# The embedding of an early-fusion kernel: positions and image products ahead of the feature products, epsilon on ScalarE, a fourth group of gathers at the start, large loads behind the first gathers

## The reference

```python
# image tokens: 16x16 patches of x, a product, the bias, a position
patches = conv(pixel_values, conv_w, strides=(16, 16)) + conv_b
h_image = patches + pos_table[pos_ids]
# text tokens: eight numbers of a table by token, powers 0 to 4 of them, a product, a position
x = turns[input_ids]                       # 8 numbers for each token
powers = x[..., None] ** arange(5)         # 40 features for each token
emb = einsum('bstp,tpd->bsd', powers, poly_coeffs) + pos_table[:s]
h_text = (emb - mean(emb)) * rsqrt(var(emb) + 1e-12) * ln_gamma + ln_beta
h = concatenate([h_image, h_text], axis=1)
# what follows begins with a normalization of every token
xn = (h - mean(h)) / sqrt(var(h) + 1e-5)
```

## Time and profile before

| | us |
|---|---|
| median of three runs (1141.53 to 1149.68) | 1148.24 |
| the profiled execution, its own time | 1145.32 |
| its span on the core | 1143.4 |
| end of the embedding in it | 95.0 |
| first instruction of the next stage in it | 95.3 |

### The profile page before, as it was taken

How to read it: one execution, slowest core, us unless ns; L and a number is a source line. 1 busy time by engine, 2 the same in 40 slices (tenths; PEclk the granted TensorE clock), 3 DMA queues, 4 the chain that set the end, 5 groups by cost and what they waited for, 6 DMA issues and landing times. The chain is left out here.

```text
span 1143.4 us, 22929 instructions
## 1 busy us (share of the span) xinstructions
PE 748.7 (65%) x6119; PEld 519.3 (45%) x6120; DVE 948.8 (83%) x2473; ACT 778.6 (68%) x1335; POOL 162.6 (14%) x271
## 2 busy tenths in 40 slices
PE   4761167765888456666666666666643298799997
PEld 3641023533555233333333333333322186688996
DVE  5876878787888799999999999999999872476676
ACT  0342045875888789999999999999974065345553
POOL 5840030006554000000000000000000740000000
PEclk9995579997999778787787777777755687899999
DMA  5001000001111111001010000000003000455542
GB/s 163 3 2 69 0 0 1 0 0 29 36 36 37 38 23 22 21 21 21 21 22 21 21 21 21 21 21 21 14 6 145 11 1 1 178 186 179 199 174 100
DMA packets 84368, 54.59 MB, mean 48 GB/s; under 512 B 53832, under 2 KB 83304, under 8 KB 84072
## 3 DMA queue, kind: packets, MB, share of 16 engines
q1 hardware_dynamic: 83304, 53.97, 15.4%
q0 software_dynamic: 1024, 0.13, 0.2%
HBM read 11.77 MB, written 3.76 MB: 14 GB/s over the span
## 5 line engine op out<-in xcount | busy, mean ns | idle before, releaser
L1281 DVE SCALAR_TENSOR_TENSOR expo<-expo,con,pow 128x153 f32<-128x153 f32 x480 | 146.1, 376 | 0.7 <-ACT expo L1215 0.7
L1110 PE MATMUL at_pT<-identb,vi 128*128 128x128 bf16 x480 | 62.8, 299 | 88.4 <-ACT vi L1189 87.9
L1094 PE MATMUL at_rem<-below,identb 128*128 128x459 bf16 x160 | 68.2, 426 | 61.6 <-ACT expo L1215 60.9
L1215 ACT ACTIVATE expo<-at_rem,con 128x459 f32<-128x459 f32 x160 | 96.7, 641 | 15.3 <-PE at_rem L1095 7.6
L923 DVE TENSOR_REDUCE rs_ends<-rs_banks 128x770 f32 (+1 forms) x96 | 91.2, 959 | 15.9 <-PE rs_banks L894 14.9
L843 ACT ACTIVATE rs_banks<-rs_banks 128x770 f32<-128x770 f32 x96 | 76.4, 798 | 26.5 <-PE rs_banks L886 25.0
L1178 ACT ACTIVATE octave<-at_banks,con 128x459 int16<-128x459 f32 x160 | 90.2, 652 | 1.3 <-PE at_banks L749 0.2
L744 PE MATMUL at_banks<-pick,row_top 128*128 128x459 bf16 x160 | 78.4, 490 | 18.7 <-ACT octave L1178 17.0
L1330 DVE CUSTOM_DVE_ANT_0 weight_top<-weight_top,line 128x2448 uint16<-128x2448 uint16 x64 | 83.8, 1350 | 8.3 <-ACT line L1206 5.2
L1110 PEld LDWEIGHTS at_pT<-identb,vi 128*128 128x128 bf16 x480 | 44.3, 133 | 102.0 <-issue 76.4
L1306 DVE TENSOR_TENSOR expo<-expo,inv_total 128x1224 f32<-128x1224 f32 x64 | 83.6, 1347 | 0.0
(11 more groups left out here) (390 smaller groups left out, 2217.1 us busy)
## 6 DMA issues: line engine op xcount, KB each, us to landing
qk<-vt SPq DMA_DIRECT2D x64, 384.0 KB, 3.1
rs_kb<-qk SPq DMA_DIRECT2D x128, 28.7 KB, 2.0
kb<-qk SPq DMA_DIRECT2D x128, 28.7 KB, 1.9
patches<-in_patches SPq DMA_DIRECT2D x4, 768.0 KB
vi<-vt SPq DMA_DIRECT2D x32, 96.0 KB, 2.0
out<-vi SPq DMA_DIRECT2D x32, 96.0 KB, 1.8
pj_w<-in_w SPq DMA_DIRECT2D x1, 2304.0 KB, 8.1
qb<-qk SPq DMA_DIRECT2D x128, 6.0 KB, 1.8
```

What stands on the lines that cost most here:

```text
L1094: pe.matmul(out, identb[:, :], bank(below, b), start=True, stop=False)
L1110: mm = pe.transpose(pT[:, slot, j * P:(j + 1) * P], src, identb[:, :])
L1215: act.activation(bank(ex, b), rem[:, (u + b) % 2, 0:3 * N], ACT.Square, bias=c(5)).then_inc(sq_done, 1)
L1281: ins = v.scalar_tensor_tensor(ex[:, t, :], ex[:, t, :], c(7), pw[:, t, :].bitcast(BF16), ALU.add, ALU.mult, accum_out=tot[:, t:t + 1])
```

## The change

Six edits, all inside `embed`:

1. The accumulator of the embedded text has four slots and not three. To make room, the image product and the transposed features share one bank of PSUM, `pfirst`.
2. TensorE's embedding(g) runs image product, both position products, the two transposes, then both coefficient products. For g = 0 the image product comes last.
3. The epsilons are added on ScalarE, by a new step variance, and not on GpSimd. GpSimd keeps the powers and waits for variance.
4. ScalarE's order is feature(g+1), collect(g-2), variance of the first kind (g), variance of the second kind (g-1), normalize(g-1).
5. GpSimd gathers four groups ahead and not three.
6. SyncE issues the loads from `wimg` on only when the first group's gathers have landed. VectorE clears `vi` behind the image bias and not ahead of the first features.

```diff
-    HALVES = 3
+    HALVES = 4
...
-        pimg, pfeat = k.ps("pimg", [P, 512], F32, st), k.ps("pfeat", [P, 512], F32, st)
+        pfirst = k.ps("pfirst", [P, 512], F32, st)
+        pfeat, pimg = pfirst[:, 0:2 * P], pfirst[:, 2 * P:2 * P + C]
+        small = sb("small", [P, 2])
...
+                sp.wait_ge(gathered[0], 64)
                 sp.dma_start(wimg[:, :, :], d["wimg"]).then_inc(in_wimg, 16)
...
                 def root1(g):
-                    pool.wait_ge(aggr1, 4 * g + 4)
-                    pool.tensor_scalar(var1[:, g, 0:4], mv1[:, g, :, 1], 1e-12, None, ALU.add).then_inc(var1_ok, 1)
                     pool.wait_ge(var1_ok, g + 1)
...
+                AHEAD = 4
+                for g in range(AHEAD):
                     gather(g)
...
+                def image(g):
                     if g == 0:
                         pe.wait_ge(in_wimg, 16)
...
                     if g > 0:
                         pe.wait_ge(img_out, g)
                     for kt in range(KI):
...
+                def embedding(g):
+                    pair = lambda half: pemb[:, emb_slot(g, half), 0:2 * C]
+                    if g > 0:
+                        image(g)
                     for half in range(2):
 
                         before = 2 * g + half - HALVES
                         if before >= 0:
                             pe.wait_ge(scaled_ok, 2 * before + 2)
...
+                        pe.matmul(pair(half), ident[:, :], postxt[:, :], start=True, stop=False)
+
+                    pe.wait_ge(feat_ok, g + 1)
+                    if g > 0:
+
+                        pe.wait_ge(featT_sb, g)
+                    for h in range(2):
+                        mm = pe.transpose(pfeat[:, h * P:(h + 1) * P], feat[:, 4 * g + 2 * h:4 * g + 2 * h + 2, :].rearrange("p b f -> p (b f)"), ident[:, :])
+                    mm.then_inc(featT_ps, 1)
+                    pe.wait_ge(featT_sb, g + 1)
+                    for half in range(2):
+                        pe.matmul(pair(half), featT[:, g % 2, half * P:(half + 1) * P], coef[:, :], start=False, stop=True).then_inc(emb_acc, 1)
+                    if g == 0:
+                        image(g)
...
+                def variance(g, mean_var, out, tokens, eps, aggr, done):
+
+                    act.wait_ge(aggr, tokens * g + tokens)
+                    act.activation(out[:, g, 0:tokens], mean_var[:, g, 0:tokens, 1], ACT.Identity, bias=small[:, eps:eps + 1]).then_inc(done, 1)
+
                 feature(0)
+                act.wait_ge(feat_set, 5)
                 for g in range(G):
                     if g + 1 < G:
                         feature(g + 1)
-                    if g > 0:
-                        normalize(g - 1)
                     if g > 1:
                         collect(g - 2)
+                    variance(g, mv1, var1, 4, 0, aggr1, var1_ok)
+                    if g > 0:
+                        variance(g - 1, mv2, var2, 5, 1, aggr2, var2_ok)
+                        normalize(g - 1)
...
-                v.memset(m["vi"][:, :, :], 0.0)
...
+                v.memset(m["vi"][:, :, :], 0.0)
+                v.wait_ge(feat_set, 6)
```

More of the change, by code:

```diff
@@ L142, in root2 @@
                 def root2(g):
-                    pool.wait_ge(aggr2, 5 * g + 5)
-                    pool.tensor_scalar(var2[:, g, :], mv2[:, g, :, 1], 1e-5, None, ALU.add).then_inc(var2_ok, 1)
                     pool.wait_ge(var2_ok, g + 1)
                     pool.tensor_tensor(rstd2[:, g, :], var2[:, g, :], power[:, g, :], ALU.pow).then_inc(rstd2_ok, 1)
-                for g in range(3):
+                AHEAD = 4
+                for g in range(AHEAD):
                     gather(g)
@@ L154, in _ @@
                         root2(g - 1)
-                    if g + 3 < G:
-                        gather(g + 3)
+                    if g + AHEAD < G:
+                        gather(g + AHEAD)
                 root2(G - 1)
@@ L162, in _ @@
                 pe.wait_ge(in_emb, 64)
-                def embedding(g):
-                    pe.wait_ge(feat_ok, g + 1)
-                    if g > 0:
-                        pe.wait_ge(featT_sb, g)
-                    for h in range(2):
-                        mm = pe.transpose(pfeat[:, h * P:(h + 1) * P], feat[:, 4 * g + 2 * h:4 * g + 2 * h + 2, :].rearrange("p b f -> p (b f)"), ident[:, :])
-                    mm.then_inc(featT_ps, 1)
+                def image(g):
                     if g == 0:
@@ L179, in embedding @@
                     for kt in range(KI):
-                        mm = pe.matmul(pimg[:, 0:C], patches[:, kt, g * P:(g + 1) * P], wimg[:, kt, :], start=(kt == 0), stop=(kt == KI - 1))
+                        mm = pe.matmul(pimg, patches[:, kt, g * P:(g + 1) * P], wimg[:, kt, :], start=(kt == 0), stop=(kt == KI - 1))
                     mm.then_inc(img_acc, 1)
-                    pe.wait_ge(featT_sb, g + 1)
+                def embedding(g):
+                    pair = lambda half: pemb[:, emb_slot(g, half), 0:2 * C]
+                    if g > 0:
+                        image(g)
                     for half in range(2):
@@ L188, in embedding @@
                             pe.wait_ge(scaled_ok, 2 * before + 2)
-                        pair = pemb[:, emb_slot(g, half), 0:2 * C]
-                        pe.matmul(pair, featT[:, g % 2, half * P:(half + 1) * P], coef[:, :], start=True, stop=False)
-                        pe.matmul(pair, ident[:, :], postxt[:, :], start=False, stop=True).then_inc(emb_acc, 1)
+                        pe.matmul(pair(half), ident[:, :], postxt[:, :], start=True, stop=False)
[10 more added lines that the diff above has]
+                        image(g)
                 def turn(g):
@@ L217, in feature @@
                         act.wait_ge(emb_acc, 2 * g - 2)
-                    act.activation(featT[:, g % 2, :], pfeat[:, 0:2 * P], ACT.Copy).then_inc(featT_sb, 1)
+                    act.activation(featT[:, g % 2, :], pfeat, ACT.Copy).then_inc(featT_sb, 1)
                 def normalize(g):
@@ L241, in _ @@
                         feature(g + 1)
-                    if g > 0:
-                        normalize(g - 1)
                     if g > 1:
                         collect(g - 2)
+                    variance(g, mv1, var1, 4, 0, aggr1, var1_ok)
+                    if g > 0:
+                        variance(g - 1, mv2, var2, 5, 1, aggr2, var2_ok)
+                        normalize(g - 1)
+                variance(G - 1, mv2, var2, 5, 1, aggr2, var2_ok)
+                collect(G - 2)
                 normalize(G - 1)
-                collect(G - 2)
                 collect(G - 1)
@@ L255, in _ @@
                 v.memset(power[:, :, :], -0.5).then_inc(feat_set, 1)
+                v.memset(small[:, 0:1], 1e-12).then_inc(feat_set, 1)
+                v.memset(small[:, 1:2], 1e-5).then_inc(feat_set, 1)
                 v.memset(m["vt"][:, :, :], 0.0)
-                v.memset(m["vi"][:, :, :], 0.0)
-                v.wait_ge(feat_set, 3)
+                v.wait_ge(feat_set, 5)
                 def features(g):
@@ L280, in image @@
                     v.wait_ge(img_acc, g + 1)
-                    v.tensor_tensor(Hres[:, B + g, :], pimg[:, 0:C], convb[:, :], ALU.add).then_inc(img_out, 1)
+                    v.tensor_tensor(Hres[:, B + g, :], pimg, convb[:, :], ALU.add).then_inc(img_out, 1)
                 def statistics2(g):
@@ L306, in _ @@
                 v.tensor_tensor(convb[:, :], convb[:, :], posimg[:, :], ALU.add).then_inc(feat_set, 1)
-                v.wait_ge(feat_set, 4)
+                v.memset(m["vi"][:, :, :], 0.0)
+                v.wait_ge(feat_set, 6)
                 for g in range(G):
```

## The result

| | before | changed |
|---|---|---|
| median, us | 1144.9 | 1191.04 (1190.1 to 1196.48) |
| ratio of changed to before, 95% interval | | 1.0408 [1.0372, 1.0443] |
| span of the profiled execution | 1143.4 | 1189.6 |
| embedding ends at | 95.0 | 142.5 |
| what stands behind the embedding | 1048.4 | 1047.1 |

All of the loss is in the embedding, which is 47.5 us longer; what stands behind it takes 1.3 us less than before.

The account below looks back on a forecast made before the run. No engine is full, so order and waits bound the kernel. A closed chain between powers (+32.7 us) and low TensorE clock (+10.1) make 42.8 on 1145.32: 1188, range 1173 to 1201, chance 0.73.

Parts of the forecast that it names:

- The path, 13.21 us at full clock: Embedding loop: a chain from one power to the next through all four engines, 13.21 us a group against 8.24.
- What closes the loop: TensorE: the single `pimg` makes image product(g+1) wait for VectorE's image(g), closing the chain between powers; no size of its own.
- The clock, +10.1 us: TensorE bursts start at low clock after 6.75 us gaps: five groups by 1.81 and 1.03 for the last turn.
- The start, first power at 25.5: Before the loop: held loads put the image bias at about 16.7, so GpSimd's first power starts at 25.5 us.
- First to second power, 11.0: First period of the embedding loop, which holds no turn: 11.0 us, putting the second power at 36.5.
- The end: Behind the last power the old order nearly holds, 15.5 us; the embedding ends at 127.7 against 95.0 at full clock.
- The base: The 42.8 us were added to the profiled execution's 1145.32, 2.9 under the median 1148.24; on the median, 1191.
- Full clock throughout: Rival: same chain between powers, TensorE never at low clock; +32.7 us, 1178, or 1175 at the earliest; chance 0.12.
- all low: Rival: same chain, TensorE at low clock through the whole burst, positions too; +50.6 us, 1196, late start 1200; chance 0.11.
- The open path: Rival: variance(g) on ScalarE starts at once, GpSimd is relieved, not slower; -7 us, some 1138 to 1141; chance 0.04.
- 2.2 us behind collect each time: Reading of the old trace: TensorE's turn waits 2.2 us for ScalarE's collect each time, 18.1 us over six turns.
- 13 to 15: Sign to look for: root1's powers on GpSimd 13 to 15 us apart in groups 2 to 6.

Follow-up runs that it names:

- the run with the gap filled: Changed kernel plus 18 identity products that nothing reads, behind TensorE's coefficient products, to fill its idle gap; 1184.5 us, ratio 1.0347.

## Why the prediction was right

The forecast was 1188, measured 1191.04; the path that it named is the one in the trace, and of its two links, the additions on ScalarE and the late transposes, one cut alone gives back all of the loss and the other nearly three quarters. The size is closer than its terms: a path taken too long and a tail that came out shorter hid part of a clock term that was too small. By its own steps:

- **The path, 13.21 us at full clock.** 12.96 in the run with the gap filled. Collect was taken at 1.48 with its hand-over and is 1.22 here (84.04 to 85.26), since variance needs no hand-over to another engine first. Feature was taken at 0.38 and lets collect start after 0.28 (83.76 to 84.04). Variance to power, unseen before, is 85.26 to 85.64, 0.38 against 0.32.
- **What closes the loop.** The prediction said that it is the image product's wait for image(g), which the single `pimg` makes. That is so for the first two groups only (22.46 and 33.70 wait for L297). In the steady turn image(g) is done 0.4 us before turn begins and 2.6 us before the image product does; the loop closes because turn(g-2), which waits for normalize, stands ahead of the image product in TensorE's list. The sum went over turn all the same, so no number hangs on it.
- **The clock, +10.1 us.** Right in kind, too small. Each of the five bursts starts low, behind gaps of 5.0 to 6.2 us where 6.75 was forecast. Turn takes 2.19 us (76.12 to 78.31) and not 1.11, 1.08 more. The image product took 3.74 here and on average over the five groups 3.25, 1.30 more than 1.95; I had used 0.78, from the product at 38.39 of the kernel before, and in that one the clock came back half-way:

```profile
38.30:39.50 1.20, 1.20 (x6) 1.20 (x5) 0.28 (x1) 0.38 (x1) 1.11 (x2) 0.50 0.08 3
...
39.50:41.10 1.60, 1.60 (x10) 1.60 (x9) 1.60 (x6) 0.00 (x0) 1.34 (x3) 0.85 0.00 0
```

  With these, five groups by 2.38 and 1.08 make 13.0, and the mean period 15.29 less 2.38 is 12.91, the full-clock path again.
- **The start, first power at 25.5.** It came at 27.72. The bias was at 18.22 and not 16.7 (my own terms, 7.4 + 2 + 2 + 4.7, add up to 16.1, so it was 2.1 late against them). The image product behind it took 2.76 us (22.46 to 25.22) and not 1.95, while the granted clock reads 1.00 there; the runs don't say why. Features(0) did come early, at 9.76, but nothing that binds followed from it.
- **First to second power, 11.0.** 12.05; the image product at 33.70 took 3.53 to the positions, and I had left this one at full clock. That is 1.6 more; features, statistics and image(1) took 0.7 less than my 2.84.
- **The end.** From power to end 16.0 against 15.5. The embedding ends 4.7 us after my 137.8: the clock is 2.9 more, the start 2.2, the first period 1.1, the end 0.5; the path is 1.5 less over five periods and group 7 0.4 less, which makes 4.8 with the rounding.
- **The base.** The 1188 stands on the profiled execution, 1145.32; on the median of three runs it would have been 1191, and the median of all four is 1144.9. The spans of the profiled executions differ by 46.2 and I had 42.8: the 4.7 us above, less 1.3 that came off behind the embedding.
- **The rivals.** Full clock throughout is out, the windows show 0.50 in every turn; all low is out too, positions and transposes run at 1.00. The open path exists, but not in the changed kernel: with the transposes first and variance at the head of ScalarE's turn the time is 1140.37, in the 1138 to 1141 that this rival gave. Moving one variance alone does not open it (1165.59).
- **Readings.** Turn does not stand 2.2 us behind collect each time: the six waits that make up 18.1 are 1.5 to 2.2 us and one of 8.1. The powers were 14.6 to 15.9 us apart, not 13 to 15.

That the two edits do more together than their sum is shown by the square of runs: neither 1141.14, late transposes alone (with the shared bank) 1145.68, additions on ScalarE alone 1156.76, both 1191.04. Apart they cost 4.5 us, hardly clear of the noise, and 15.6 us, together 49.9. Each of the four also holds collect ahead of normalize, the fourth group of gathers and the held loads.

What stays open: why the image product took 3.4, 2.5, 3.7, 2.7 and 3.8 us in the five groups. It is all that makes the periods alternate between about 14.6 and 15.8, since what is left of each is 12.0 to 12.1; the runs don't say what decides it.

## What to carry to other kernels

Before moving an operation to an engine with time to spare, write down what stands ahead of it in that engine's list, and what that in turn waits for: a step of 0.3 us on ScalarE here inherited the waits of feature and collect. Two edits that look independent, one that makes a step late and one that puts another behind it, must be costed as one. And where a wait closes a loop over several engines, the idle gap that it makes on TensorE can be paid again in clock, here 2.4 us of a period of 15.3.

## What the runs showed of the hardware

- In the changed kernel TensorE ran every turn at 1.2 GHz after idle gaps of 5.0 to 7.9 us, and the last one after 3.62 us. Gaps of 2.1 to 2.2 us went either way. In the kernel before the turn at 62.20 ran at 2.4 GHz, and the one at 70.44 began at 1.00 and fell to 0.51 within 0.6 us (70.40 to 70.70, 70.70 to 71.00). In the run with 18 products four turns behind such gaps ran at 2.4 GHz and one, at 95.38, fell to 1.2. Gaps of 3.63 us went either way too: with variance at the head, the first four transposes took 1.12 us at 72.31 (clock 0.50) and 0.66 at 84.15 (clock 1.00).
- With a low clock in the loop the time of a group does not add up from its parts alone: a head start of 0.86 us shrank to 0.26 in one group and to 0.12 by the seventh power. This change of less than a microsecond upstream could not be read at the end.
- A float32 product with 128 columns stands in the trace as two records 0.11 us apart at full clock: 36 records for 18 products, 4.18 us (63.22), and 8.0 us for 36 products.
